# Norms, first pass: VectorE's two adds of the experts' results become accumulating transfers issued by GpSimd

## What is computed

```
x1   = graph convolution of x + x @ W_res + biases
core = top-2 mixture of 64 experts of x1      # two gated rows of 256 per node
y    = x1 + core
mean = mean(y, axis=0);  var = mean((y - mean)**2, axis=0)
h    = (y - mean) * rsqrt(var + 1e-5) * gamma + beta
out  = layernorm(x + h)                        # over the 256 values of each row
```

## Time and profile before

| | us |
|---|---|
| median of 3 runs | 3553.36 (3551.93 to 3555.17) |
| the profiled execution's own time | 3556.91 |
| its span, first to last instruction | 3555.2 |
| `norms` begins | 3343.2 |
| last product of the first pass ends | 3446.6 |

### The profile page before, as it was taken

The page is one execution under the profiler, slowest core; times in us unless marked ns, Lnnn a source line. Parts: engine busy times, 40 slices in busy tenths (PEclk is TensorE's granted clock), DMA queues, the critical chain, the costliest instruction groups (busy, mean ns, idle before and its releaser), DMA issues. The chain is left out here.

```text
span 3555.2 us, 59150 instructions
## 1 busy us (share of the span) xinstructions
PE 2821.7 (79%) x14820; PEld 1978.5 (56%) x14953; DVE 1915.3 (54%) x6500; ACT 1137.3 (32%) x2723; POOL 2086.0 (59%) x2177
## 2 busy tenths in 40 slices
PE   3755888888888888888888888877999999999550
PEld 3532445444444444545444444446899889889440
DVE  6993444454445444444544444545555555555587
ACT  3970122222122212122221212223444444444238
POOL 3005777777777777777777777753555555555300
PEclk8877999999999999999999999998999999999775
DMA  8616444444444444444444444434444544444477
GB/s 348 260 43 206 124 135 134 123 134 125 136 134 124 134 123 135 134 126 134 123 134 135 126 134 123 123 112 142 154 130 143 168 142 137 142 154 131 147 237 227
DMA packets 288801, 522.32 MB, mean 147 GB/s; under 512 B 44699, under 2 KB 189982, under 8 KB 285968
## 3 DMA queue, kind: packets, MB, share of 16 engines
q0 software_dynamic: 102048, 274.24, 28.2%
q1 hardware_dynamic: 183888, 207.62, 18.0%
q10 hardware_dynamic: 2720, 38.64, 2.6%
HBM read 404.64 MB, written 120.48 MB: 148 GB/s over the span
## 5 line engine op out<-in xcount | busy, mean ns | idle before, releaser
L1167 POOL DMA_INDIRECT work<-h_table,src_cols x1661 | 1573.4, 947 | 728.3 <-issue 500.8
L1487 PE MATMUL ps<-work 128*128 128x257 f32 x3322 | 1093.3, 411 | 351.7 <-DMA work<-h_table,src_cols 330.1
L1487 PEld LDWEIGHTS ps<-work 128*128 128x128 f32 x3322 | 540.3, 190 | 853.6 <-issue 564.7
L1187 DVE TENSOR_TENSOR work<-rel_cols,ps 128x1152 f32<-128x1152 f32 x196 | 251.2, 1283 | 1033.8 <-PE ps L1487 1033.4
L1384 PE MATMUL ps<-none_w,none 128*128 128x512 bf16 x1271 | 485.3, 382 | 0.0
L1622 POOL DMA_INDIRECT picked<-ys,places x232 | 254.8, 1098 | 358.7 <-DVE ys L1692 341.7
L1739 PEld LDWEIGHTS ps<-xst,work 128*128 128x128 f32 x3648 | 443.5, 193 | 28.6 <-issue 16.6
L1739 PE MATMUL ps<-xst,work 128*128 128x128 f32 x3648 | 447.5, 276 | 11.4 <-issue 10.6
L1746 PE MATMUL ps<-work,hid 128*128 128x256 f32 x1824 | 436.4, 383 | 3.5 <-ACT hid L1603 3.1
L1603 ACT ACTIVATE hid<-ps,b_cols 128x128 f32<-128x128 f32 x912 | 314.8, 367 | 169.9 <-PE ps L1739 126.5
L1746 PEld LDWEIGHTS ps<-work,hid 128*128 128x128 f32 x1824 | 329.4, 191 | 48.6 <-ACT hid L1603 13.5
(11 more groups left out here) (271 smaller groups left out, 3489.9 us busy)
## 6 DMA issues: line engine op xcount, KB each, us to landing
work<-in_L_gnn_w_dram SPq DMA_DIRECT2D x128, 512.0 KB, 4.6
work<-h_table,src_cols POOLq DMA_INDIRECT x1661, 2.8
picked<-acc ACTq DMA_DIRECT2D x1, 25088.0 KB, 102.0
pk<-picked SPq DMA_DIRECT2D x14, 1792.0 KB, 8.3
m_base<-acc ACTq DMA_DIRECT2D x1, 12642.0 KB, 36.9
acc<-m_base SPq DMA_DIRECT2D x14, 903.0 KB, 5.8
x_rows<-acc SPq DMA_DIRECT2D x98, 129.0 KB, 3.6
x_beta<-xr_x SPq DMA_DIRECT2D x98, 128.0 KB, 1.9
```

Source lines behind the costliest of these rows:

```text
L1167: pool.indirect_dma_start(out=got[:, c % RING, 0:D], out_offset=None, in_=h_table[:, :], in_offset=bass.IndirectOffsetOnAxis(ap=src_cols[: ...
L1187: nc.vector.tensor_tensor(hot[:, (2 * t + h) % HOTS, 0:b - a, :], rel_cols[:, a:b].unsqueeze(2).broadcast_to([P, b - a, P]), lanes.unsquee ...
L1487: mm = nc.tensor.matmul(ps_flat[:, bank(t, k, w[0])], hot[:, (2 * t + (k >= HALF)) % HOTS, k % HALF if k >= HALF else k, :], got[:, c % RI ...
```

## The change

SyncE no longer loads `picked` into `pk`. GpSimd issues, for every group, two transfers from `picked` with an add as their operation: one for the first row of each node, one for the second. Each adds what it reads to `group(g)` in SBUF. The second of a group is issued once the first has landed; two groups of first transfers are issued ahead. VectorE keeps only the subtraction of the mean and waits for the second transfer. `load_x` for the first four groups waits for nothing any more, and the load of gamma comes first. ScalarE's squares now wait for `sq_used` of the group four before, a wait that SyncE's load had held.

```diff
             @block.sync
-                rows = picked.rearrange("(n k) d -> n (k d)", k=TOP_K)
-                for g in range(NG):
-                    if g >= B:
-                        sp.wait_ge(sq_used, g - B + 1)
-                        sp.wait_ge(second_added, g - B + 1)
-                    sp.dma_start(pk[:, g % B, :, :], rows_of(rows, g)).then_inc(pk_in[g % B], 16)
-                    if g == B - 1:
-                        sp.dma_start(gamma_b[:, :], ...).then_inc(gamma_in, 16)
...
+                sp.dma_start(gamma_b[:, :], ...).then_inc(gamma_in, 16)
                 for q in range(B):
-                    sp.wait_ge(second_added, NG - B + q + 1)
                     load_x(q)
...
+            @block.gpsimd
+            def _(pool):
+                rows = picked.rearrange("(n k) d -> n k d", k=TOP_K)
+                def add_rows(g, k, done):
+                    pool.dma_start(group(g), rows[g * GT * P:(g + 1) * GT * P, k, :].rearrange("(t p) d -> p t d", p=P),
+                                   accum_op=ALU.add).then_inc(done[g % B], 16)
+                for g in range(NG + 2):
+                    if g < NG:
+                        add_rows(g, 0, first_in)
+                    if g >= 2:
+                        pool.wait_ge(first_in[(g - 2) % B], 16 * ((g - 2) // B + 1))
+                        add_rows(g - 2, 1, second_in)
...
             @block.vector
-                def add_first(g):
-                    dve.wait_ge(pk_in[g % B], 16 * (g // B + 1))
-                    nc.vector.tensor_tensor(group(g), group(g), pk[:, g % B, :, 0:D], ALU.add).then_inc(first_added, 1)
-
-                def add_second(g):
-                    dve.wait_ge(first_added, g + 1)
-                    nc.vector.tensor_tensor(group(g), group(g), pk[:, g % B, :, D:2 * D], ALU.add).then_inc(second_added, 1)
...
                 def centre(g):
                     dve.wait_ge(mean_set, 1)
-                    dve.wait_ge(second_added, g + 1)
+                    dve.wait_ge(second_in[g % B], 16 * (g // B + 1))
...
                 for g in range(NG):
-                    add_first(g)
-                    if g > 0:
-                        centre(g - 1)
-                    add_second(g)
-                centre(NG - 1)
+                    centre(g)
...
             @block.scalar
                 for g in range(NG):
                     act.wait_ge(centred, g + 1)
+                    if g >= B:
+                        act.wait_ge(sq_used, g - B + 1)
                     nc.scalar.activation(pk[:, g % B, :, 0:D], group(g), ACT.Square).then_inc(squared, 1)
```

More of the change, by code:

```diff
@@ L1781, in norms @@
         last_ones_set = sem2("last_ones_set")
-        pk_in = [sem2(f"pk_in{b}") for b in range(B)]
         xb_in = [sem2(f"xb_in{b}") for b in range(B)]
@@ L1786, in norms @@
         mean_set = sem2("mean_set")
-        first_added = sem2("first_added")
-        second_added = sem2("second_added")
+        first_in = [sem2(f"first_in{b}") for b in range(B)]
+        second_in = [sem2(f"second_in{b}") for b in range(B)]
         centred = sem2("n_centred")
@@ L1821, in _ @@
             def _(sp):
-                rows = picked.rearrange("(n k) d -> n (k d)", k=TOP_K)
-                for g in range(NG):
-                    if g >= B:
-                        sp.wait_ge(sq_used, g - B + 1)
-                        sp.wait_ge(second_added, g - B + 1)
-                    sp.dma_start(pk[:, g % B, :, :], rows_of(rows, g)).then_inc(pk_in[g % B], 16)
-                    if g == B - 1:
-                        sp.dma_start(gamma_b[:, :], gamma.rearrange("(a d) -> a d", a=1).broadcast_to([P, D])).then_inc(gamma_in, 16)
                 def load_x(q):
@@ L1841, in store @@
                     sp.dma_start(out[(NT - 1) * P:N, :], pk[0:LAST, held(g), GT - 1, 0:D]).then_inc(o_out[held(g)], 16)
+                sp.dma_start(gamma_b[:, :], gamma.rearrange("(a d) -> a d", a=1).broadcast_to([P, D])).then_inc(gamma_in, 16)
                 for q in range(B):
-                    sp.wait_ge(second_added, NG - B + q + 1)
                     load_x(q)
```

## The result

The changed kernel takes 3603.3 us (median of 4 runs, 3601.8 to 3605.1) against 3552.6 beside it: a ratio of 1.0144, 95% interval 1.0132 to 1.0156, so 50.7 us slower. The forecast was +81 us with a range of 3575 to 3740.

What follows compares the result with a forecast made beforehand. VectorE and the transfers were both near their limit in the first pass of `norms`; with adding transfers, 2.8 + 162 + 11 + 8.8 = 184.7 us against 103.4 gives +81 us, 3635 us, range 3575 to 3740.

Steps and rivals of the forecast that it cites:

- The price of an adding row: First pass of `norms`: an adding 1 KB row reads twice, 2 x 51.7 = 103 ns per engine, 162 us for 1568 rows.
- B: First pass, the forecast's case: two full reads, 94 to 123 ns a row, +66 to +112 us, 3619 to 3665; chance 0.50.
- C: First pass, rival: partly overlapped reads, 56 to 94 ns a row, +7 to +66 us, 3560 to 3619; chance 0.15.
- The loads of x + beta: First four loads, moved to the block's start with gamma: take 11 us from the transfer engines and gain nothing.
- The sign that they land in the first 15 us: Expected in the new profile: the loads of x + beta land in the first 15 us.
- The issue: GpSimd's issue of 896 adding rows: costs nothing below 5.8 us; bounded at 0.95 to 6.6 us, 13.3 if reads are written twice.
- D: First pass, rival: GpSimd's issue becomes the bound, 6.63 + 0.30 us each, +105 us, 3658; chance 0.17, far end 0.03.
- The tail: After the last landing: one centring 2.0, one square 1.7, one group's products 5.0 us, 8.8 with gaps.
- The rule given there for the clock: A TensorE that idles more than half of the time gets the 1.2 GHz level; it costs 1.7 us once.
- The sum: First pass: start 2.8, adds 162, loads of x + beta and gamma 11, tail 8.8: 184.7 against 103.4 us, +81.
- The value of VectorE's relief: First pass: relieving VectorE alone, with transfers as cheap as now, brings at most some 20 us of the 103.4.
- Rival A: First pass: second read free, 44.8 to 51.7 ns a row, 0 to -10 us, 3543 to 3553, decided at 47 ns; chance 0.10.

## Why the prediction was right, and what it mis-sized

- **The direction and its cause were right.** The transfers were near their limit before, an add costs them nearly a second copy's time, and VectorE's relief is worth less than that. Copies against adds, 97.2 against 153.9 us, show it. That the extra time is a second read is argued, not shown.
- **The price of an adding row is the mis-sized term.** The prediction took "2 x 51.7 = 103 ns"; it is 82.7. The doubling was right for what it doubled: 51.7 was a packet's own time, and an adding packet takes 102.4. The step that failed is to use that as the engine's time. Adding packets overlap, 1.24 under way in an engine on average, and an engine finishes one every 82.7 ns. Its reason for 51.7 over 46.9, that a row costs more on GpSimd's queue, compared the two measures; copies cost 46.7 on either queue. Over 1568 rows, 103.4 against 82.7 ns is 32.5 us, a little more than the 30 us by which +81 overshot.
- **Which case it was.** The forecast's own case, B, had 94 to 123 ns and 3619 to 3665 us, and missed both. 3603.3 us and 82.7 ns fall into C, partly overlapped reads, which had a chance of 0.15; the stated range reached far enough down to hold it. What overlaps is whole packets; whether the two reads of one row do is not shown.
- **The loads of x + beta**: 11 us predicted, 11.2 measured by moving them. The sign that they land in the first 15 us was wrong: they shared the engines with the adds and landed by about 3370, 30 us in.
- **The issue** was to stay under 5.8 us. It is 1.6 to 1.8 us for most adds of 896 rows, and 0.93 for a copy. GpSimd waited 88.5 us of the pass; D had no part. The Trainium skill's page "DMA: Bandwidth & Descriptors", section "Anatomy of one DMA — SWDGE (gpsimd) path", calls this cost small and slow to grow with the number of descriptors. The traces agree, with 0.93 us for a copy of 896 rows beside 0.947 for an indirect issue of 128; the add's issue is longer, with a median of 1.71.
- **The tail** was put at 8.8 us with the last products at the lower clock. It was 7.1: they ran in 3.30 us, as before. The rule given there for the clock isn't borne out. TensorE was busy 73.3 of 154 us, less than half, yet the last products had the 2.4 GHz level (granted clock 1.00 from 3490 to 3494). Just before them 28 products ran without a pause for 8.9 us, with a granted clock of 0.50 up to 3486 and 0.93 from there to 3490.
- **The sum with measured terms** is 2.8 + 129.7 + 11.2 + 7.1 = 150.8 against 153.9 us; the other 3 us are the start, where the rate climbs, and gaps at the end. They were not separated.
- **The value of VectorE's relief** was called at most some 20 us; it is 24.9. The limit had been set with 366 GB/s, where an unbroken stream of 2 KB pieces reaches 385, and it put the tail behind the last transfer.
- **Rival A** needed 47 ns a row. Copies in place of the adds, at 46.7, gave a pass of 97.2 us, 6 us less than before: just under the 7.1 us that the prediction took as the least that can be told from no change.

## What to carry to other kernels

An add in a transfer is not free: here it took 1.8 to 1.9 times the engine time of a copy of the same bytes. Before moving an elementwise add from a compute engine into a transfer, look at the share of the transfer engines in that stage. Here it was 0.81, and an add of 896 rows took 2.0 us from VectorE and cost the engines 4.6 us, while it slowed the plain loads beside it. A price per row comes from a rate with the engines full; a packet's own time, read from a queue's share, is longer wherever packets overlap. And a load moved to the front of a stage is only free if the transfers don't bound the stage. When a compute engine waits for loads and the loads wait for buffers, try one more buffer first: it brought 7 us of the pass here.

## What the runs showed of the hardware that was not expected

- An add from SBUF to SBUF is slower than one from HBM to SBUF, 167 against 198 GB/s, although plain copies move 335 and 351.
- An add doubles a packet's own time, from 51.0 to 102.4 ns at 1 KB and from 88.7 to 178.5 at 2 KB, while the rates fall by less, 1.77 and 1.85 times.
- GpSimd's direct copies of 1 KB rows go out in packets of several rows, mean 16.44 MB / 4298 = 3.8 KB, and SyncE's in packets of one row, 17.52 MB / 17,422 = 1.0 KB. Both move 351 GB/s. The adding rows go out one to a packet, 25.69 MB / 25,536.
- An issue by GpSimd of 896 rows takes 0.93 us as copies and most often 1.6 to 1.8 us as adds.
